# Mixing and the second projection of a four-layer graph network joined in one stage

## The reference, cut to what matters

```python
# layer 1, end of its second step (Xf, Xa are 2048 x 512)
Z = Z + (Xf @ U1_1 + Xa @ U2_1)
Y = X + Z
layer1 = (Y - mean(Y)) * rsqrt(var(Y) + eps) * gamma + beta
x = x + layer1
h = maximum(layernorm(x), 0)
# layer 2, its first lines (8 heads of 64 columns)
Wh = einsum('nf,hfd->hnd', h, W)
e_src = einsum('hnd,hd->hn', Wh, a1)
e_dst = einsum('hnd,hd->hn', Wh, a2)
e = leaky_relu(e_src[:, :, None] + e_dst[:, None, :], 0.2)
```

## Time and profile before

| what | value |
|---|---|
| runs of the kernel before | 4431.7, 4422.23, 4430.83 us, median 4430.83 |
| the profiled execution | 4422.61 us, its span 4420.9 us, mean granted PE clock 0.896 |
| busy share of the span | PE 81%, DVE 81%, ACT 58%, POOL 32% |
| mix_stage | 2558.24 us (its first DMA) to 2659.9 us (ACT's last copy) |
| project_stage | 2662.67 us (its first DMA) to 2746.8 us (DVE's last operation) |

### The profile page before, as it was taken

One profiled execution on the slowest core, in us unless ns is written; L12 is line 12 of the kernel. 1 busy time (PEld: TensorE's weight loads), 2 busy tenths in 40 slices (PEclk: granted clock), 3 DMA queues, 4 the chain that ended last, 5 costly groups with the idle time before them and its releaser, 6 DMA issues. The chain is left out here.

```text
span 4420.9 us, 57188 instructions
## 1 busy us (share of the span) xinstructions
PE 3594.9 (81%) x20136; PEld 2089.4 (47%) x20136; DVE 3569.1 (81%) x5868; ACT 2552.1 (58%) x3032; POOL 1418.0 (32%) x1417
## 2 busy tenths in 40 slices
PE   6788888879888837888797887988887878888887
PEld 3688888534344313333343443767663423333333
DVE  4799999669999994999999552888874069999896
ACT  3656666459889873788787622544443344444442
POOL 0444100017788782599889520000002000000000
PEclk9899999989998879999898998999998988888888
DMA  4611000211110102311101061000002111111110
GB/s 154 236 26 31 26 26 21 82 44 49 41 43 30 33 14 78 118 41 34 29 22 36 19 219 51 18 15 18 15 18 67 71 53 57 43 47 44 43 43 15
DMA packets 158709, 228.81 MB, mean 52 GB/s; under 512 B 85137, under 2 KB 96288, under 8 KB 152624
## 3 DMA queue, kind: packets, MB, share of 16 engines
q1 hardware_dynamic: 147056, 191.33, 13.3%
q0 software_dynamic: 11376, 33.76, 2.1%
HBM read 158.48 MB, written 66.47 MB: 51 GB/s over the span
## 5 line engine op out<-in xcount | busy, mean ns | idle before, releaser
L1590 DVE SCALAR_TENSOR_TENSOR junk<-expd,mid 128x2048 bf16<-128x2048 f32 x440 | 1036.3, 2355 | 13.8
L578 ACT ACTIVATE steepz<-s1b,thr_h 128x1024 bf16<-128x1024 f32 (+1 forms) x768 | 665.2, 926 | 537.5 <-DVE mask L661 461.8
L721 PE MATMUL acc<-V,mask 128*128 128x198 bf16 (+1 forms) x5504 | 753.4, 276 | 182.6 <-DVE mask L663 182.6
L1490 ACT ACTIVATE junk_s<-expd,nmid 128x2048 bf16<-128x2048 f32 x264 | 528.9, 2003 | 126.6 <-POOL nmid L1550 112.7
L721 PEld LDWEIGHTS acc<-V,mask 128*128 128x128 bf16 x5504 | 484.4, 100 | 241.9 <-DVE mask L663 140.7
L1493 ACT ACTIVATE junk_s<-expd,nmid 128x2048 bf16<-128x2048 f32 x264 | 528.1, 2001 | 0.0
L1963 PE MATMUL psS<-KT,qs 64*128 64x512 f32 x1024 | 382.3, 738 | 155.8 <-DVE m L2073 151.6
L728 PE MATMUL acc<-V,adjT 128*128 128x99 bf16 (+1 forms) x5504 | 453.4, 221 | 0.0
L661 DVE TENSOR_TENSOR mask<-steepz,adjT 128x1024 bf16<-128x1024 bf16 (+1 forms) x768 | 397.8, 553 | 28.2 <-PE acc L721 16.0
L728 PEld LDWEIGHTS acc<-V,adjT 128*128 128x128 bf16 x5504 | 369.2, 99 | 51.1 <-issue 3.1
L1362 PE MATMUL psX<-parts,block 128*128 128x512 bf16 x1536 | 364.1, 393 | 12.0 <-DMA block<-adj_dram 12.0
(11 more groups left out here) (280 smaller groups left out, 5813.1 us busy)
## 6 DMA issues: line engine op xcount, KB each, us to landing
rows<-in_adj_dram SPq DMA_DIRECT2D x32, 1024.0 KB, 4.9
s1b<-sT_dram SPq DMA_DIRECT2D x32, 512.0 KB
block<-adj_dram SPq DMA_DIRECT2D x32, 512.0 KB, 4.4
adj_dram<-adjT POOLq DMA_DIRECT2D x4, 2048.0 KB, 20.2
rel_table<-zeros POOLq DMA_DIRECT2D x64, 128.0 KB, 19.6
y_dram<-yo SPq DMA_DIRECT2D x32, 256.0 KB, 2.1
step_dram<-xo SPq DMA_DIRECT2D x32, 256.0 KB, 2.0
A<-step_dram SPq DMA_DIRECT2D x8, 1024.0 KB, 13.5
```

The source lines that it names most:

```text
L578: act.activation(steepz[:, m % RELUS, :], s1b[:, q % 4, :], ACT.Relu, bias=thr_h[:, u, 1, j:j + 1], scale=STEEP).then_inc(relu_ready, 1)
L721: mm = pe.matmul(acc[:, c % 2, i // TB, o:o + 2 * W], mask[:, j % RING, tile(i)], V[:, u, j, 0:2, :].rearrange("p s w -> p (s w)"), start= ...
L1490: act.activation(junk_s[:, 0, :], expd[:, slot[i], :], ACT.Relu, bias=col(nmid, i), accum_out=col(above, i)).then_inc(sums_ready, 1)
L1590: link(dve.scalar_tensor_tensor(junk[:, :], e, col(mid, i), e, ALU.is_gt, ALU.mult, accum_out=col(mass, i)))
```

## The change: what it does

`mix_stage` and the call of `project_stage` for layer 2 become one stage, `mix_project_stage`, with the work of both (the tables of factors are now opened ahead of it). PE does the product of tile t with W thirteen iterations (BEHIND = LAG + 4) behind the turning of tile t, at the end of iteration t + 13; the scores in iterations 18, 20, 22 and 25, into `psO` once mixing has left it; and the turning of the scores into a part of `psT` in iteration 26, so the loop has 29 iterations in place of 25. ACT copies the scores and the products at the end of its own iteration of the same number. SP issues the loads of W, a1 and a2 behind `xt` of tile 3. DVE folds one of the eight pairs in each of its iterations 6 to 13, at the end of the iteration, and takes the highest scores in four reductions over 512 columns and one over four, where there was one over 2048. The arithmetic is otherwise the same. In the diff some buffers and all new semaphores are left out, and so are the steps of DVE that are those of lines 405 to 414 (both marked "...").

```diff
--- before.py
+++ after.py
@@ -1633,7 +1633,8 @@
                         dve.wait_ge(low_ready, m + 1)
                         keep(decided[m], ALU.is_ge)
 
-    def mix_stage(self, nat, tr, u2_dram, nat_dram, y_dram, x_dram, x_new, adj_in):
+    def mix_project_stage(self, nat, tr, u2_dram, nat_dram, y_dram, x_dram, x_new, adj_in, H, DH, w_dram, a1_dram,
+                          a2_dram, g):
 
         nc, a = self.nc, self.a
         with self.open() as st:
@@ -1649,7 +1650,19 @@
             veps = self.sb(st, "veps", [P, 2])
             sd = self.sb(st, "sd", [P, 2])
             rstd = self.sb(st, "rstd", [P, 2])
+            wp = self.sb(st, "wp", [P, KD, D])
+            avec = self.sb(st, "avec", [P, 2, H, DH])
...
             psT = self.ps(st, "psT", [P, 2, KD, P])
+            psQ = self.ps(st, "psQ", [P, 2, D])
             psO = self.ps(st, "psO", [P, 2, D])
             norm = RowNorm(self, st, nat, tr)
             w_in = self.sem(st, "w_in")
@@ -1666,7 +1679,25 @@
             x_ready = self.sem(st, "x_ready")
             v_ready = self.sem(st, "v_ready")
             sd_ready = self.sem(st, "sd_ready")
...
             dve_done = self.sem(st, "dve_done")
+            psS = psT[:, 0, :, :].rearrange("p k i -> p (k i)")[:, 0:NT * 2 * H].rearrange("p (t h) -> p t h", t=NT)
+            BEHIND = LAG + 4
+            scored = {18: 0, 20: 1, 22: 2, LAG + NT: 3}
             block = st.enter_context(nc.Block())
 
             @block.sync
@@ -1683,6 +1714,12 @@
                     if t >= 4:
                         sp.wait_ge(x_ready, t - 3)
                     sp.dma_start(xt[:, t % 4, :], x_dram[tile(t), :]).then_inc(x_in[t % 4], 16)
+                    if t == 3:
+                        for k in range(KD):
+                            sp.dma_start(wp[:, k, :].rearrange("p (h d) -> p h d", h=H),
+                                         w_dram[:, tile(k), :].rearrange("h p d -> p h d")).then_inc(wp_in, 16)
+                        for i, v in enumerate((a1_dram, a2_dram)):
+                            sp.dma_start(avec[:, i, :, :], v.partition_broadcast(P)).then_inc(a_in, 16)
                     if t < 3:
                         c = t + 1
                         sp.dma_start(nat[:, 4 * c:4 * c + 4, :],
@@ -1690,6 +1727,13 @@
                                      ).then_inc(nat_in[c], 16)
                 for c in range(4):
                     sp.dma_start(self.adjT[:, 4 * c:4 * c + 4, :], self.adj_dram[:, 4 * c:4 * c + 4, :]).then_inc(adj_in, 16)
+                sp.wait_ge(sT_copied, 4)
+                sp.dma_start(g.sT_dram[0:2 * H, :], sT[:, :]).then_inc(sT_out, 16)
+                sp.wait_ge(top_ready, 1)
+                sp.dma_start(g.top_dram[0:2 * H].rearrange("(h o) -> h o", o=1), top[:, :]).then_inc(top_out, 16)
+                sp.wait_ge(top_out, 16)
+                sp.dma_start(m2[:, :], g.top_dram[H:2 * H].partition_broadcast(P)).then_inc(m2_in, 16)
+                sp.wait_ge(sT_out, 16)
 
             @block.gpsimd
             def _(pool):
@@ -1706,7 +1750,30 @@
 
             @block.tensor
             def _(pe):
-                for t in range(NT + LAG):
+                def sequence(t):
+                    if t == 0:
+                        pe.wait_ge(wp_in, 16 * KD)
+                    pe.wait_ge(norm.n_copied, t + 1)
+                    if t >= 2:
+                        pe.wait_ge(seq_copied, t - 1)
+                    for k in range(KD):
+                        mm = pe.matmul(psQ[:, t % 2, :], tr[:, k, tile(t)], wp[:, k, :],
+                                       start=(k == 0), stop=(k == KD - 1))
+                    mm.then_inc(seq_ready, 1)
+
+                def scores(c):
+                    if c == 0:
+                        pe.wait_ge(w12_ready, 1)
+                        pe.wait_ge(o_read, NT)
+                    pe.wait_ge(norm.n_copied, 4 * c + 4)
+                    if c >= 2:
+                        pe.wait_ge(sT_copied, c - 1)
+                    for k in range(KD):
+                        mm = pe.matmul(psO[0:2 * H, c % 2, :], w12[:, k, :, :].rearrange("p i h -> p (i h)"),
+                                       tr[:, k, c * D:(c + 1) * D], start=(k == 0), stop=(k == KD - 1))
+                    mm.then_inc(sT_ready, 1)
+
+                for t in range(NT + BEHIND):
                     if t < NT:
                         if t % 4 == 0:
                             pe.wait_ge(nat_in[t // 4], 16)
@@ -1723,12 +1790,22 @@
                         pe.wait_ge(y_in[u % 4], 16 * (u // 4 + 1))
                         pe.matmul(psO[:, u % 2, :], self.ident[:, :], yt[:, u % 4, :], start=False,
                                   stop=True).then_inc(o_ready, 1)
-                    if t >= LAG:
+                    if LAG <= t < NT + LAG:
                         norm.turn(pe, t - LAG)
+                    if t in scored:
+                        scores(scored[t])
+                    if t >= BEHIND:
+                        sequence(t - BEHIND)
+                    if t == NT + BEHIND - 3:
+                        pe.wait_ge(sT_copied, 4)
+                        pe.wait_ge(t_copied, NT)
+                        for u in range(NT):
+                            mm = pe.transpose(psS[:, u, :], sT[:, tile(u)], self.ident[0:2 * H, 0:2 * H])
+                        mm.then_inc(s_ready, 1)
 
             @block.scalar
             def _(act):
-                for t in range(NT + LAG + 1):
+                for t in range(NT + BEHIND):
                     if t < NT:
                         act.wait_ge(t_ready, t + 1)
                         act.copy(tr[:, :, tile(t)], psT[:, t % 2, :, :]).then_inc(t_copied, 1)
@@ -1740,8 +1817,22 @@
                         norm.root(act, (t - 7) // 4)
                     if LAG - 1 <= t < NT + LAG - 1:
                         norm.relu(act, t - LAG + 1, xo[:, (t - LAG + 1) % XO, :])
-                    if t >= LAG + 1:
+                    if LAG + 1 <= t < NT + LAG + 1:
                         norm.copy(act, t - LAG - 1)
+                    if t in scored:
+                        c = scored[t]
+                        act.wait_ge(sT_ready, c + 1)
+                        act.copy(sT[:, c * D:(c + 1) * D], psO[0:2 * H, c % 2, :]).then_inc(sT_copied, 1)
+                    if t >= BEHIND:
+                        u = t - BEHIND
+                        act.wait_ge(seq_ready, u + 1)
+                        act.copy(nat[:, u, :], psQ[:, u % 2, :]).then_inc(seq_copied, 1)
+                act.wait_ge(args_ready, 1)
+                act.activation(g.colE[:, :, :], d2[:, :, :], ACT.Exp, bias=shift[:, 0:1])
+                act.activation(g.rowE[:, :, :], cmin[:, :, :], ACT.Exp)
+                act.activation(g.rowF[:, :, :], cmax[:, :, :], ACT.Exp)
+                act.activation(ftmp[:, :, :], d2[:, :, :], ACT.Exp, bias=shift[:, 0:1],
+                               scale=SLOPE).then_inc(exps_ready, 1)
 
             @block.vector
             def _(dve):
@@ -1771,6 +1862,16 @@
                     dve.wait_ge(x_ready, t + 1)
                     norm.moments(dve, link, t, xo[:, t % XO, :])
 
+                def fold(n):
+                    k, i = n // 2, n % 2
+                    if n == 0:
+                        dve.wait_ge(wp_in, 16 * KD)
+                        dve.wait_ge(a_in, 32)
+                    link(dve.tensor_tensor(prod[:, :].rearrange("p (h d) -> p h d", h=H),
+                                           wp[:, k, :].rearrange("p (h d) -> p h d", h=H), avec[:, i, :, :], ALU.mult))
+                    link(dve.tensor_reduce(w12[:, k, i, :], prod[:, :].rearrange("p (h d) -> p h d", h=H),
+                                           AX.X, ALU.add))
+
                 for t in range(NT + 4):
                     if t < NT:
                         look(t)
@@ -1778,6 +1879,31 @@
                         finish(t - 1)
                     if t >= 6 and (t - 6) % 4 == 0:
                         norm.scale(dve, link, (t - 6) // 4)
+                    if 6 <= t < 6 + 2 * KD:
+                        fold(t - 6)
+                    if t == 6 + 2 * KD:
+                        dve.memset(shift[:, :], SHIFT).then_inc(w12_ready, 1)
+                for c in range(4):
+                    dve.wait_ge(sT_copied, c + 1)
+                    last = dve.tensor_reduce(tops[:, c:c + 1], sT[:, c * D:(c + 1) * D], AX.X, ALU.max)
+                link(last)
+                dve.tensor_reduce(top[:, :], tops[:, :], AX.X, ALU.max).then_inc(top_ready, 1)
+                dve.wait_ge(s_ready, 1)
+                dve.tensor_copy(s[:, :, :, :].rearrange("p t i h -> p t (i h)"), psS).then_inc(s_copied, 1)
+                dve.wait_ge(s_copied, 1)
+                dve.wait_ge(m2_in, 16)
...
+                dve.wait_ge(exps_ready, 1)
+                dve.tensor_scalar(g.colF[:, :, :], ftmp[:, :, :], -1.0, None, ALU.mult)
 
     def top_p_stage(self, natA, trA, natB, trB, xa_dram, xT_dram, kq_dram, parts_dram, y_dram):
 
```

(48 more changed lines are left out.)

## The result

The changed kernel takes 4411.51 us (median of 10 runs, 4405.16 to 4419.06), the kernel before 4425.24 us (median of 10, 4422.23 to 4434.4). The ratio is 0.9966 with a 95% interval from 0.9957 to 0.9974: 15 us less, between 11.5 and 19 (the two medians by themselves differ by 13.7). I had forecast 4408, with 4400 to 4420 as range. In the profiled executions the span fell from 4420.9 to 4403.5 us.

The account below looks back on a forecast made before the run. PE was taken to bound both stages, with over 20 us of little or no work between. Terms: 22.8 - 1.4 - 0.5 - 2.0 - 0.2 = 18.7 us less, from 4426.8 to 4408 us, range 4400 to 4420.

Parts of the forecast that it names:

- rivals 1 and 2: Rival 1, and a second one: W's load and DVE's lag both hidden, saving 21.2 us, time 4405.6, chance 0.15.
- rival 1: Mixing from tile 6: folding products wait for POOL, DVE sets the pace; PE held about 4 us, time 4411.6, chance 0.15.
- my own signs: PE without gaps over 1 us but two, clock 1.00, 8.6 us per late tile, attention 18 to 19 us earlier.
- the two waits named: The only PE gaps over 1 us allowed for: at `yt` of tile 4 and ahead of the fourth scores.
- Idle time and turns: Between the stages: PE's idle 11.0 us go, eight turns take 3.4 us in place of 12.2; gain 19.8 us.
- Clock: Start of the products: PE no longer stops, so the low granted clock there goes; gain 3.0 us.
- One exchange with ACT: Fourth block of scores, iteration 25: PE waits for two ACT copies and hand-overs; cost 1.4 us.
- Folding on DVE: Iterations 6 to 13: eight pairs make DVE lag 3.3 us, slack about equal; cost 0.5 us, bounds 0 and 3.3.
- W's load in SP's queue: Tile 4 of mixing: six DMAs ahead of its `yt` make it land late; cost 2.0 us, bounds 0 and 8.
- Rival 4: SP's queue holds W's loads by pieces, PE stands at tile 4 for some 95 us; time 4504, chance 0.03.
- Clearing: From PE's end to the attention: more semaphores to clear; cost 0.2 us, bounds 0 and 1.2.
- rival 3: PE waits behind ACT's product copy in each of 16 iterations, losing 22 us: no change, 4427, chance 0.05.

## Why the prediction was right, and where its terms were off

The time, 4411.5, lies in the range, and the sign is the one forecast. That says less of the terms than it seems: the range of 20 us takes in rivals 1 and 2 as well, the measured time is the very 4411.6 that I gave rival 1 a chance of 0.15 for, and that too is partly luck, since its base was 1.6 us high and its saving, 15.2, is 1.4 less than the profile's. Of my own signs, the clock at 1.00 and the two waits named came; against them stand a gap of 1.32 us at tile 11, products of 1.9 us, and the attention 16.9 us earlier instead of 18 to 19. Term by term, against the 16.6 us of the profile:

- *Idle time and turns, 19.8 us: right.* PE's row of products follows its turns without a gap. The runs split the idle time: load 7.2, barrier 3.8. The turns are the other 8.8; with the products last PE waits for ACT at them again.
- *Clock, 3.0 us: right, but 2.8 in size.* The granted clock is at 1.00 from 2573 us to the end of the products. I had taken the distance of two copies, 3.43 us, off the 6.40; from its own start to ACT's copy a product at full clock takes 3.63. Kept as two stages, the first product still lost 5.99 - 3.63 = 2.4.
- *One exchange with ACT, 1.4 us: right.* 1.16 us of wait and a hand-over; 1.27 us came back when the scores were put behind the product (168.85 to 167.58).
- *Folding on DVE, 0.5 us taken: wrong, 3.4 us.* Tiles 11, 12 and 13 come 1.51, 0.99 and 0.89 us later than their work asks. This is the step that failed. I had the row that shows the wait, and priced it as my first rival, "about 4 us", beside the rule of the Trainium skill (page "SBUF — State Buffer", Who interferes with whom) that a DVE instruction with both inputs in SBUF is blocked in full by a GpSimd instruction that reads SBUF and began first, but took the other case for likelier because DVE "might well begin first, by a tenth of a microsecond". It did begin first in the record, by 0.09 us, and it lost all the same.
- *W's load in SP's queue, 2.0 us taken: 0.8.* The mechanism was right. The timeline of SP in the kernel after:

```profile
2573.25 10.29 SPq L1719 DMA_DIRECT2D wp<-in_L_gnn_W_dram  x4
2583.59 1.89 SPq L1722 DMA_DIRECT2D avec<-in_L_gnn_a_dram  x2
2585.51 0.43 SPq L1713 DMA_DIRECT2D yt<-y_dram  x1
```

  The four loads held SP for 10.29 us where they had taken 4.33 with nothing ahead of them; so the y of tile 4 was issued at 2585.5, not 2588, and PE got it 0.54 us late (0.8 by the distances of tiles 3 to 5, 5.43 and 4.84 us where 4.73 is the rule). Rival 4, a hold that grows with the number of pieces, is out: 2.6 us for a load of 1024 pieces.
- *Clearing, 0.2 us: it was -0.2.*
- *Not in the sum at all, about 0.9 us.* A block of scores between other work costs PE more than 3.43 us. In a row, four took 13.91 us before; standing alone, each has a longer step on both sides, in PE's timeline after:

```profile
2668.38 0.60 PE L154 MATMUL psN<-ident,A 128*128 128x128 f32 x4
2668.91 3.61 PE L1772 MATMUL psO<-B,w 128*16 128x512 f32 x8
2672.45 3.70 PE L1760 MATMUL psQ<-wp,B 128*128 128x512 f32 x8
2675.99 0.60 PE L154 MATMUL psN<-ident,A 128*128 128x128 f32 x4
```

  The steps are 0.53 (a turn is 0.43), 3.54 and 3.54 us: 0.3 us a block, four times, where before it came once.

So 22.6 - 1.3 - 3.4 - 0.8 + 0.2 - 0.9 = 16.4; the y of tile 0 came 0.1 us sooner than before, and 0.1 is rounding. Rivals 1 and 3 were the two that put a wait on ACT's rows: rival 1 is what happened at tiles 11 to 13; rival 3 (ACT's order) is out, since with DVE in time PE waits at the one place named.

The base was off too. I read four runs of the kernel before as two levels. Ten runs, from 4422.2 to 4434.4 with five of them between 4423.9 and 4426.3, show one level with a tail upwards; that the mean that I took, 4426.8, lay only 1.6 us above their median was luck. In the profiles the kernel ahead of the stage took 2555.35 to 2561.25 us, though its code is the same, and what follows it 1672.3 to 1677.0: this scatter is larger than any single term but the main ones.

## What to carry to other kernels

When stages are joined, the gain is what the bounding engine did not do between them (load, barrier, turns at another engine's pace, low clock), and it can be read off one timeline; the losses come from work that was hidden in the old stage and now meets other company. Place each moved operation in the tile's time, not only on its engine: here a product with two SBUF inputs cost 0.69 or 1.94 us depending on its place beside POOL's addition, and moving it by one position won 3.2 us. And give a moved step a deadline: folding too late cost more than folding in the wrong place.

## What the runs showed of the hardware that I had not expected

DVE's product was recorded to begin 0.09 us ahead of POOL's addition (2611.53 and 2611.62) and still waited for all of it, 1.94 us in place of 0.69, and so did every product with such a lead. With POOL's zeros ahead of the addition the product went first all eight times: six times with a recorded lead of 0.19 to 0.49 us, but twice with 0.01 us or less (2616.75 and 2616.76), each time behind a small operation of DVE that is recorded 0.08 us ahead of the addition; POOL's addition then took 1.33 to 1.81 us in place of 1.27. So leads between 0 and 0.1 us in the record do not tell who holds up whom; why is open. The Trainium skill's page "SBUF — State Buffer" (Who interferes with whom) says that the later one of such a pair is blocked in full. The lengths agree; that the later one loses can't be read from the recorded starts, at a lead of 0.09 us. POOL's writing of zeros, 0.33 us, left a product beside it at 0.69, as that page has it for an instruction that only writes.

The same four DMAs of W held SP for 4.33 us with nothing ahead of them, for 3.98 behind the x of tile 6, and for 10.3 us behind the x of tile 3, where the queue was some 10 us behind the earlier trace rows. What SP issues behind them waits as long: the y of tile 4 was issued at 2585.51 us, and at 2573.56 in the kernel before.
